# Scores with keys on the lanes, and split weights kept in memory

## The reference

```
xh = layernorm(x)                                   # (4, 256, 512)
q = (xh @ Wq + bq)                                  # 32 heads of 128, in 8 groups of 4
k, v = split(ctx @ Wkv + bkv)                       # 8 key and 8 value heads of 128
attn = softmax(q . k / sqrt(128)) over the 1601 keys
x = x + tanh(g_xattn) * ((attn @ v) @ Wo + bo)
x = x + tanh(g_ffn) * (base(layernorm(x)) + 2 * routed low-rank experts, the top 2 of 8)
```

## Time and profile before

| | |
|---|---|
| median of three runs | 2658.36 us (2652.68 to 2659.72) |
| the profiled execution | 2655.5 us |
| its span, first to last instruction | 2653.7 us |
| granted TensorE clock, mean | 0.986 |
| DMA | 129.06 MB, mean 49 GB/s |

### The profile page before, as it was taken

One profiled execution on the slowest core, in us unless ns is written; L12 is line 12 of the kernel. 1 busy time (PEld: TensorE's weight loads), 2 busy tenths in 40 slices (PEclk: granted clock), 3 DMA queues, 4 the chain that ended last, 5 costly groups with the idle time before them and its releaser, 6 DMA issues.

```text
span 2653.7 us, 39006 instructions
## 1 busy us (share of the span) xinstructions
PE 2556.9 (96%) x15464; PEld 2270.3 (86%) x15464; DVE 1520.8 (57%) x2813; ACT 1215.3 (46%) x2515; POOL 748.4 (28%) x1098
## 2 busy tenths in 40 slices
PE   7999999998999999999799999999989999999998
PEld 7889898987888989898788988989878898988985
DVE  6665656555465565656455565565644656556575
ACT  4544545444444454545344444454534545445450
POOL 3223223226231322223522222321443223232210
PEclk9999999999989999999899999999989999999999
DMA  4111111113121111111211111111221111111121
GB/s 135 44 40 44 41 30 51 37 48 86 45 50 36 39 45 42 44 35 55 75 55 47 33 45 45 39 44 42 59 68 55 42 34 46 39 47 40 36 72 36
DMA packets 128440, 129.06 MB, mean 49 GB/s; under 512 B 45057, under 2 KB 116993, under 8 KB 127874
## 3 DMA queue, kind: packets, MB, share of 16 engines
q1 hardware_dynamic: 128258, 126.58, 18.0%
HBM read 122.74 MB, written 3.80 MB: 48 GB/s over the span
## 4 chain that ended last, share of the span: by engine, by line
PE 83%; DMA 9%; POOL 3%; DVE 2%; ACT 2%; issue 1%; SPq 0%; POOLq 0%; DVEq 0%
PE psW L451 18%; PE psW L328 12%; PE psW L251 11%; PE psW L252 11%; PE psW L253 11%; PE psS L253 6%; PE psS L251 6%; PE psS L252 6%; DMA scr_r<-rinv 3%; DMA stg<-in_ctxT 3%; ACT p_sb L644 1%; POOL cl L595 1%; ACT pth L607 1%; PE psW L375 1%; DMA stg<-in_wo 1%
## 5 line engine op out<-in xcount | busy, mean ns | idle before, releaser
L757 DVE TENSOR_TENSOR ptl<-psW,pth 128x512 fp32r<-128x512 f32 (+1 forms) x1024 | 567.6, 582 | 408.7 <-ACT pth L607 404.0
L644 ACT ACTIVATE p_sb<-psS,nm 128x802 f32<-128x802 f32 (+1 forms) x512 | 473.2, 932 | 482.9 <-DVE nm L805 435.6
L607 ACT ACTIVATE pth<-psW 128x512 fp32r<-128x512 f32 (+1 forms) x1024 | 499.3, 515 | 328.3 <-PE psW L328 327.1
L328 PE MATMUL psW<-ident,p_sb 128*128 128x128 f32 (+1 forms) x3328 | 450.7, 276 | 49.0 <-DVE on L1043 42.4
L328 PEld LDWEIGHTS psW<-ident,p_sb 128*128 128x128 f32 (+1 forms) x3328 | 390.7, 141 | 97.2 <-DVE on L1043 44.0
L797 DVE TENSOR_REDUCE mx<-psS 128x1 f32<-128x802 f32 (+2 forms) x576 | 374.3, 705 | 44.9 <-PE psS L253 41.4
L251 PE MATMUL psS<-kl,qh 128*128 128x512 f32 (+2 forms) x1024 | 365.4, 357 | 0.7 <-ACT p_sb L644 0.7
L253 PE MATMUL psS<-kh,ql 128*128 128x512 f32 (+2 forms) x1024 | 355.3, 347 | 0.0
L252 PE MATMUL psS<-kh,qh 128*128 128x512 f32 (+2 forms) x1024 | 352.8, 345 | 0.0
L451 PE MATMUL psW<-pth,vh 128*128 128x512 f32 (+1 forms) x832 | 341.3, 410 | 0.0
L593 POOL TENSOR_SCALAR wqh<-stg 128x342 fp32r<-128x342 f32 (+1 forms) x192 | 94.0, 490 | 860.4 <-PE psW L253 765.9
(11 more groups left out here) (142 smaller groups left out, 4348.1 us busy)
## 6 DMA issues: line engine op xcount, KB each, us to landing
stg<-in_wq SPq DMA_DIRECT2D x128, 171.0 KB, 2.4
stg<-in_wo SPq DMA_DIRECT2D x128, 171.0 KB, 2.4
rbc<-scr_r SPq DMA_DIRECT2D x64, 256.0 KB, 4.7
stg<-in_wq SPq DMA_DIRECT2D x64, 170.0 KB, 2.4
stg<-in_wo SPq DMA_DIRECT2D x64, 170.0 KB, 2.4
stg<-in_wk SPq DMA_DIRECT2D x62, 128.0 KB, 4.8
stg<-in_ctxT SPq DMA_DIRECT2D x36, 201.0 KB, 2.4
stg<-in_wv SPq DMA_DIRECT2D x32, 171.0 KB, 4.2
```

The source lines that it names most:

```text
L328: m = eng.transpose(o[0:rows, (t - g) * 128:(t - g + 1) * 128], p_sb[:, i % 2, 128 * t:128 * t + rows], ident[:, :])
L607: return eng.activation(hi, src, ACT.Copy)
L644: eng.activation(p_sb[:, i % 2, lo:hi], psS[:, OFF + lo:OFF + hi], ACT.Exp, bias=nm[:, i % 2:i % 2 + 1], accum_out=sums[:, i // 4 % 2, i % ...
L757: return eng.tensor_tensor(lo, src, f32(hi), ALU.subtract)
```

## The change

**Scores with the keys on the lanes.** A tile of 128 keys is stationary and the unit's 512 query columns stream: 13 tiles by three matmuls of 512 columns in place of 48 matmuls. The exponentials come out with keys on the lanes, as the product with V wants them, so `turn_p`, `upper_p` and `lower_p` go.

**Maximum and sum over lanes.** The maximum of a query now runs over lanes. ScalarE copies each score tile to `xs` (21 tiles), VectorE keeps a running maximum `mrun` of the tiles. After 13 tiles TensorE turns `mrun` (4 turnings, job "m"), VectorE reduces it to `nm`, SyncE writes it to memory (`scr_m`) and reads it back as a broadcast `mb`. GpSimd subtracts `mb` from each kept tile; ScalarE takes the exponential twice, to PSUM in full and to `ph` rounded; VectorE makes the lower part and adds to a running sum. Tiles 1 and 2 (batches 1 to 3; in batch 0 none of them) and tile 0 go to SBUF, and there GpSimd does both. The sum is turned as well (job "s"), and its reciprocals take the way they took before.

**Slots.** All engines' loops now run over slots, one for each score tile, 13 in a unit. In slot s stand the scores of tile s, the subtraction of tile s-18, the exponentials of s-19, the product with V of s-21, and jobs from a table of four kinds of unit. VectorE does a job's part one slot later. Scores have two PSUM banks, the product with V two, the full exponentials two, and all jobs share two.

**Weights and contexts kept.** In batch 0 GpSimd cuts each weight once (`cut`), and SyncE writes both parts to memory (`keep`). From batch 1 on SyncE loads both parts (`load`). A head's Q weights have one buffer instead of a pair of heads'. Contexts of batches 1 to 3 are cut in 48 pieces ahead of time, written to memory, and loaded by chunk (`load_ctx`).

**Smaller ones.** K's chunks are 384, 384, 384 and 450 columns. The output's bias is added once a batch by VectorE (`add_bias`) in place of two one-row matmuls. After the last score three more units' worth of slots run the rest.

```diff
+    CH = [(0, 384), (384, 384), (768, 384), (1152, 450)]
+    SUB, EXP, VAL = 18, 19, 21
+    RX, RP = 21, 4
+    SLOTS = NT * (UN + 3)
+    def lead(U):
+        return 1 if U < NU else 3
+    AT = [
+        {0: "m", 1: "o0", 2: "k3", 3: "o1", 5: "q0", 6: "s", 7: "q1", 9: "v0", 11: "v1"},
+        {0: "v2 m", 1: "o0", 2: "q0", 3: "v3", 4: "o1", 5: "v4", 6: "s", 7: "v5", 8: "q1", 9: "v6", 10: "k0"},
+        {0: "m k1", 1: "o0", 3: "k2", 4: "o1", 6: "s k3", 8: "q0", 10: "q1", 11: "x0"},
+        {0: "m", 1: "o0", 2: "x1", 3: "o1", 4: "q0", 5: "k0", 6: "s", 8: "k1", 10: "q1", 11: "k2"},
+    ]
...
+            if kind == "q" and 2 * n + part + 1 < 2 * NU:
+                cuts[s + 1] += halves("q", 2 * n + part + 1)
...
         @block.tensor
-            def turn_p(i, groups=range(4)):
...
+            for s in range(SLOTS):
+                if s < TN:
...
+                    if s >= 2:
+                        pe.wait_ge(s_e, s - 1)
+                        if (s - 2) % NT or s > NT:
+                            pe.wait_ge(s_m, 12 * ((s - 2) // NT) + (s - 2) % NT)
+                    three(psS[0:rows, s % 2, :], kh[:, ks], kl[:, ks], qh[:, U % 2, :], ql[:, U % 2, :]).then_inc(s_s)
+                T = s - VAL
+                if 0 <= T < TN:
...
+                    if t < lead(U):
+                        pe.wait_ge(s_lp, lp_count[T])
+                    else:
+                        pe.wait_ge(s_l, l_count[T])
+                    eng.matmul(o, vh[0:rows, t, hs], hi, start=t == 0, stop=False)
+                    eng.matmul(o, vh[0:rows, t, hs], lo, start=False, stop=False)
+                    eng.matmul(o, vl[0:rows, t, hs], hi, start=False, stop=t == NT - 1).then_inc(s_pv)
+                for j in jobs[s]:
+                    job(*j)
...
         @block.sync
+            def load(kind, n, per_batch, used, v):
+                j = n % per_batch
+                sp.wait_ge(s_keep[kind], 32 * per_batch)
+                sp.wait_ge(used, v)
+                hi, lo = parts[kind]
+                eng.dma_start(f32(hi), scr_w[kind][j, 0]).then_inc(s_load[kind], 16)
+                eng.dma_start(f32(lo), scr_w[kind][j, 1]).then_inc(s_load[kind], 16)
...
+            for s in range(SLOTS):
...
+                for p in cuts.get(s + 1, []):
...
+                        fetch(*p)
+                for kind, n, part in cuts.get(s - 1, []):
+                    if kind == "c":
+                        keep_ctx(n)
+                    elif part == len(halves(kind, n)) - 1:
+                        keep(kind, n)
+                for kind, n, part in jobs[s]:
+                    if kind == "m":
+                        sp.wait_ge(s_nm, n + 1)
+                        eng.dma_start(scr_m[n % 2].rearrange("(t p) -> p t", p=128), nm[:, n % 2, :],
+                                      allow_slow_non_contiguous=True).then_inc(s_mw, 16)
+                        sp.wait_ge(s_mw, 16 * (n + 1))
+                        if n >= 2:
+                            sp.wait_ge(s_sub, NT * (n - 1))
+                        eng.dma_start(mb[:, n % 2, :], scr_m[n % 2].partition_broadcast(128)).then_inc(s_mb, 16)
+                    elif kind == "s":
...
+                        sp.wait_ge(s_rw, 16 * (n + 1))
...
+                    elif kind == "q" and 2 * NU <= 2 * n + part + 1 < 2 * UN:
+                        load("q", 2 * n + part + 1, 2 * NU, s_q, 2 * n + part + 1)
...
         @block.gpsimd
+            def cut(kind, n, a):
...
+                    if n:
+                        pool.wait_ge(used, v)
+                        pool.wait_ge(s_keep[kind], 32 * n)
+                pool.wait_ge(s_stg[no % 2], 16 * (no // 2 + 1))
+                eng.tensor_scalar(hi, raw, 1.0, 0.0, ALU.mult, ALU.add).then_inc(s_cut)
+                pool.wait_ge(s_cut, 2 * no + 1)
+                eng.tensor_tensor(lo, raw, f32(hi), ALU.subtract).then_inc(s_cut)
...
+            for s in range(SLOTS):
+                T = s - SUB
...
+                    pool.wait_ge(s_mb, 16 * (U + 1))
+                    pool.wait_ge(s_e, T + 1)
+                    eng.tensor_tensor(tile, tile, mb[0:rows, U % 2, :], ALU.subtract).then_inc(s_sub)
+                T = s - EXP - 1
+                if 0 <= T < TN and T % NT < lead(T // NT):
...
+                    eng.tensor_tensor(pl[:, T % RP, :], p, f32(ph[:, T % RP, :]), ALU.subtract).then_inc(s_lp)
...
+                for p in cuts[s]:
+                    cut(*p)
...
         @block.scalar
+                    upper(xs[0:rows, s % RX, :], psS[0:rows, s % 2, :]).then_inc(s_e)
...
+                    act.wait_ge(s_sub, T + 1)
...
+                    eng.activation(p, xs[0:rows, T % RX, :], ACT.Exp)
...
+                    eng.activation(ph[0:rows, T % RP, :], xs[0:rows, T % RX, :], ACT.Exp).then_inc(s_h)
...
         @block.vector
+                        eng.tensor_tensor(run, psS[0:rows, s % 2, :], a, ALU.max).then_inc(s_m)
+                for j in jobs.get(s - 1, []):
+                    after_job(*j)
...
+                    lower(pl[0:rows, T % RP, :], p, ph[0:rows, T % RP, :]).then_inc(s_l)
...
+                    eng.tensor_tensor(total, p, total, ALU.add).then_inc(s_a)
+                if t == 11 and 0 <= U - 2 < UN:
...
+                    dve.wait_ge(s_rb, 16 * (V + 1))
...
+                    eng.tensor_tensor(on[:, :], psV[:, V % 2, :], rbc[:, :], ALU.mult).then_inc(s_on)
```

More of the change, by code:

```diff
@@ new lines, in gated_block, with halves @@
+    F0 = TN + 1
+    for i in range(6):
+        jobs[F0 + 2 * i].append(("ht", i, 0))
+        jobs[F0 + 2 * i + 1].append(("mi", i, 0))
+    for i in range(4):
+        jobs[F0 + 14 + 2 * i].append(("ga", i, 0))
+        jobs[F0 + 15 + 2 * i].append(("y", i, 0))
+    def halves(kind, n):
+        return [(kind, n, a) for a in range(2 if kind in "vo" else 1)]
+    WIDTH = {"q": 512, "k": 512, "v": 512, "o": 512}
+    first = halves("q", 0) + halves("v", 0) + halves("q", 1) + halves("k", 1) + halves("o", 0)
@@ new lines, in gated_block @@
+    cuts = {s: [] for s in range(SLOTS)}
+    for s in range(SLOTS):
+        for kind, n, part in jobs[s]:
+            if kind == "q" and 2 * n + part + 1 < 2 * NU:
+                cuts[s + 1] += halves("q", 2 * n + part + 1)
+            if kind == "k" and part == 3 and n + 1 < 8:
+                cuts[s + 1] += halves("k", n + 1)
+            if kind == "v" and part == 6 and n + 1 < 4:
+                cuts[s + 1] += halves("v", n + 1)
+            if kind == "o" and part == 1 and n + 1 < NU:
+                cuts[s + 1] += halves("o", n + 1)
@@ L72, in gated_block, with cut_count @@
+    cuts[0] += halves("q", 2)
+    for b in range(1, B):
+        for n in range(16):
+            cuts[NT * (NU * (b - 1) + 3) + 9 * n + 4].append(("c", 16 * (b - 1) + n, 0))
+    order = first + [p for s in range(SLOTS) for p in cuts[s]]
+    number = {p: n for n, p in enumerate(order)}
+    def cut_count(kind, n):
+        return 2 * number[halves(kind, n)[-1]] + 2
     with ExitStack() as ctx:
@@ L236, in _ @@
             pe = Once(eng)
-            free = [(k, None, 0) for k in range(4)]
+            free = [(0, None, 0), (1, None, 0)]
             def take(key):
@@ new lines, in have_ctx, with proj_k @@
+            def have_ctx(b, c):
+                if b == 0:
+                    pe.wait_ge(s_el, 1 + 2 * (c + 1))
+                else:
+                    pe.wait_ge(s_lc[c], 32 * b)
+            def proj_k(K, c):
+                lo, w = CH[c]
+                have_weight("k", K, 8)
+                have_ctx(K // 8, c)
+                pe.wait_ge(s_pad, 2)
+                o = take(("k", K, c))
+                for k in range(KT):
+                    m = three(o[:, 0:w], wkh[:, k, :], wkl[:, k, :], ch[:, k, lo:lo + w], cl[:, k, lo:lo + w],
+                              k == 0, k == KT - 1)
+                m.then_inc(s_k)
+                emptied(("k", K, c), s_kl, 4 * K + c + 1)
@@ L481, in _ @@
+            job("ht", 6, 0)
+            job("ga", 4, 0)
+            job("y", 4, 0)
+            job("mi", 6, 0)
+            job("ht", 7, 0)
+            job("mi", 7, 0)
+            job("ga", 5, 0)
+            job("y", 5, 0)
+            for i in (6, 7):
+                job("ga", i, 0)
+                job("y", i, 0)
         @block.sync
```

1186 lines of the change are left out of this document (534 added, 652 removed).

## The result

| | before | after |
|---|---|---|
| median | 2656.7 us (4 runs, 2652.7 to 2659.7) | 3311.4 us (4 runs, 3306.4 to 3314.7) |
| span of the profiled execution | 2653.7 | 3312.3 |
| granted TensorE clock, mean | 0.986 | 0.872 |
| DMA | 129 MB | 291 MB |

The ratio is 1.246, interval 1.244 to 1.249: 25% slower. The forecast was 2794, with a range to 2950. The sign held; the size was missed by 517 us.

The account below looks back on a forecast made before the run. TensorE, busy 96%, was taken to bound the kernel. Before the first slot 33 us, units 2196, waits 483 and 82 behind the last score made 2794 us, 5.2% slower; range 2470 to 2950, the forecast case's own 2690 to 2890.

Parts of the forecast that it names:

- The trip of 13.4 us: Values written to memory and read back as a broadcast: 13.4 us, of which the write's landing 8.2, the read's 4.7.
- None of the rivals: Nothing late, 2311 us (0.12); late in part, 2553 (0.23); GpSimd binds, 3014 (0.12); no turnings spared (no chance of its own).
- my three signs of being wrong: Units under 38 us apart, the trip under 10 us, or VectorE or ScalarE busy over 85%.
- 64 units of 34.3 us: Units without waits: 33.8 us of TensorE issue plus 0.5 for light slots, 2196 us over 64 units.
- 82 behind: Behind the last score: 21 slots of about 1.9, trip 13.4, output, last two feed-forward tiles; 82 us, an estimate.
- my terms for context cuts and loads: Context cuts falling where SyncE is held, 45 us (0 to 100); new context loads ahead of weight loads, 24 us.
- 91+38+108+150: Maxima late 91; reciprocals holding the next unit's first turning 38; second head's weights behind SyncE's wait 108; batch 0 150 us.
- the clock's 27: TensorE's clock drops after waits: 1.7 us lost behind each of 16 waits of kind 2, 27 us (0 to 60).
- my count of issue: TensorE's issue in a unit of the changed kernel: 33.8 us, 4.4 less than the earlier kernel's 38.2.
- 0.5 for the light slots: Slots without a job last 1.9 us instead of 1.41, mostly hidden by heavy slots beside them: 0.5 us a unit.
- The rival began at 1.4: GpSimd binds behind the maxima: from 1.4 us a subtraction it decides; at 1.6 us, 3014 us; chance 0.12.
- my own bound, 3.5 us a unit at 1.3: Maxima's lateness, mean 1.9 us over 48 units (91 us), was bounded at 3.5 a unit if GpSimd needs 1.3.

Follow-up runs that it names:

- no_trips: The changed kernel with maxima and reciprocals replaced by constants and the trips' writes and reads not issued by SyncE; 2748.3 us.
- lean: pe_both with sums by products with a ones column, scaled context in PSUM, maxima's diagonal rounded, output products in slots 11 and 12; 2651.2 us, again 2649.4 (ratio 0.995).
- row_write: The changed kernel with each trip's 128x4 values turned by TensorE and written as 4 packets of 512 bytes instead of 512 of 4; 3013.1 us.
- pe_both: The changed kernel with both trips replaced by TensorE broadcasts (diagonals times ones), and subtraction, exponentials and product with V one slot earlier; 2826.9 us.

## Why the prediction was wrong, by its own steps

**What held.** The sign, and its reason: TensorE is spared work, and the waits outweigh it. The trip of 13.4 us: in the chain 8.12+5.98 = 14.1 and 8.55+5.03 = 13.6. Two writes a unit in SyncE's waits, 8 us each. The maxima late in most units. Q weights late, though by 216 us where I had 108. None of the rivals came, and none of my three signs of being wrong showed: two looked for a unit or a trip that is too short, and the third for a busy VectorE or ScalarE.

**The steps that failed.** Two terms of the sum were too small. The first and larger one is the kernel without its waits: 64 units of 34.3 us with 33 in front and 82 behind, 2311 us, to which my terms for context cuts and loads add 69. no_trips took 2748, 368 more. The second is the price of the trips: 91+38+108+150 = 387 us against the 563 that no_trips spares, 149 more once the clock's 27 is added to my side. 368+149 = 517, the whole miss.

**The kernel without trips.** The first and last scores of no_trips and of the changed kernel (count, ns min/median/max, first and last start us), and no_trips between them:

```profile
L329 PE MATMUL psS<-ql,kh x832: 387/396/794, 39.9 to 2598.6; 128*128 128x512 f32 x154, 128*65 128x512 f32 x13
```

```profile
L325 PE MATMUL psS<-ql,kh x832: 387/396/797, 38.9 to 3154.5; 128*128 128x512 f32 x154, 128*65 128x512 f32 x13
```

```profile
39.90:2599.80 2559.90, 2257.19 (x11680) 1888.78 (x11680) 1862.11 (x2920) 1557.65 (x2885) 1574.73 (x1319) 0.96 0.28 95
```

A unit takes 2560/64 = 40.0 us, 5.7 over my 34.3, which is 295 us over 64 units after the 69 for cuts and loads. TensorE is busy 35.3 of them, 1.5 over my count of issue, and idle 4.7, where I had put 0.5 for the light slots and 1.1 for cuts and loads. Behind the start of the last score come 148 us (158 in the changed kernel), where I had 82: that is 66 of the 368 and has nothing to do with the trips. In front of the first stand 7 more than my 33.

I had let heavy slots hide the light ones. Scores have two PSUM banks and all jobs two more, so little carries over; that this is the reason is argued, not tried. The stretched lower part belongs here only in part: it is 2.50 us in the mean in no_trips, where the constants let GpSimd run early, and 0.96 in the changed kernel. So no_trips is somewhat slower than the changed kernel would be with trips that cost nothing, and 563 is rather too low and 368 too high; TensorE's share of that is not measured. lean has 2.8 us idle a unit between its scores although it issues more. What the job table gave of this is not separated. My count of the issue spared, 280 us, is not confirmed either: TensorE's busy time fell from 2556.9 to 2368.5 in no_trips, by 188, at a clock of 0.945 instead of 0.986.

**What a trip costs.** I priced it by who waits at its end (91+38), by who stands behind SyncE's wait (108) and by batch 0 (150), as terms that add. The runs show that it does not work so: freeing the data gave nothing (3355), freeing the queue 58, both 136, and only taking the transfers away gave 563. A write of 512 packets of 4 bytes costs 6 to 8 us whichever way it is arranged. If SyncE stands until it has landed, the loads start 8 us later; if it does not, they land 6 us later (11.6 us against 5.4), whichever of two queues the write is in. The earlier trace rows had the sign of it, 2 KB in 8.2 us beside 256 KB in 4.7, and I took it for a latency instead of asking what it does to others. The form of the writes is 298 us of the 563 (row_write). The other 265 are in what a trip with short writes still costs, and that stays open.

**The clock.** I gave it 27 us, 1.7 behind each of 16 waits; no run shows the 1.7. The granted clock was 0.84 to 0.90 all through; TensorE's waits now reach 18.6 us and stand in every batch, where before the longest was 11.9. That the waits bring the low clock is argued from the earlier trace rows and this, not tried by itself. The same 12056 matmuls were 2476.0 us busy after and 2368.5 in no_trips, 107 us more. How much of that is the clock, and how much matmuls that come singly and overlap less in their records, is not separated.

**GpSimd.** A subtraction takes 1.31 us (1309 ns), not 1.1. The rival began at 1.4, so its condition was not met. By my own bound, 3.5 us a unit at 1.3 instead of 1.9, the term of 91 should have been 168. But GpSimd is busy 48% and doesn't bind: pe_both has the same subtractions and takes 485 us less.

**The range** reached to 2950 because I took my bounds term by term; none held the case that loads beside a write get slower, nor that the 34.3 itself or the 82 could be short. The sign came out right with room to spare, but not by a good sum: the kernel without any trip was already some 90 us slower than the one before, and by my terms it was to take 2380 us.

## What to carry to other kernels

Here the number of packets, and not the bytes, made a small write dear, for itself and for the loads beside it. Before small values go through memory, turn them so that they are written as rows, and ask what is loaded in those microseconds. If freeing a wait gives nothing and freeing the queue gives nothing, take the transfer away. A count of issue by slot is a floor: before you trust it, ask how far two buffers let a heavy slot carry a light one, and count what runs behind the last unit. Where VectorE works beside a busy GpSimd, keep one of its two operands in PSUM. And replace values by constants with care: the constants moved GpSimd's work and brought a delay that the changed kernel hardly had.

## What the hardware showed that I had not expected

- A load of 256 KB issued 2.2 us behind a write of 512 packets of 4 bytes took 12.69 us on the write's own queue (three other loads between) and 10.25 us on another, against 4.11 without trips. As 4 packets of 512 bytes SyncE waited 0.9 us for the write, and the load behind it took 3.78. The small packets themselves took 1.1% of the engines' time.
- VectorE's operation with two SBUF operands took up to 7.21 us beside GpSimd's subtractions, ending 0.55 us after a whole row of them; with one operand in PSUM it took 0.74.
- A reciprocal of 128x512 took 3.35 us, five times another operation of that size.
- An unrounded product of 512 columns took 1.02 us, a rounded one 0.23.
